# Reordering the handover from the shared feed-forward to the routed experts, and the order of each expert tile's steps

## The reference

```
x  = x + ((x * ys) @ weight) * d                       # ys = cond / sqrt(512)
shared = (silu(x @ w1) * (x @ w3)) @ w2                # hidden width 1024
s = sigmoid([x, cond] @ router_W);  top 2 of 8 by s + bias;  gates = s_sel / sum(s_sel)
routed = sum over the two chosen e of gate * (gelu(x @ W1e[e]) @ W2e[e])   # width 512
out = x + (shared + routed) / 3
```

## Time and profile before

| what | value |
|---|---|
| median of 3 runs (lowest, highest) | 1060.47 us (1059.27, 1061.65) |
| the profiled execution's own time | 1054.4 us |
| its span, first to last instruction | 1052.6 us |
| TensorE busy in the span | 1021.2 us, 97% |
| VectorE, ScalarE, GpSimd busy | 506.2, 293.0, 331.5 us |
| mean granted TensorE clock | 0.996 of full |

### The profile page before, as it was taken

One profiled execution on the slowest core, in us unless ns is written; L12 is line 12 of the kernel. 1 busy time (PEld: TensorE's weight loads), 2 busy tenths in 40 slices (PEclk: granted clock), 3 DMA queues, 4 the chain that ended last, 5 costly groups with the idle time before them and its releaser, 6 DMA issues.

```text
span 1052.6 us, 14602 instructions
## 1 busy us (share of the span) xinstructions
PE 1021.2 (97%) x4692; PEld 836.1 (79%) x4692; DVE 506.2 (48%) x828; ACT 293.0 (28%) x461; POOL 331.5 (31%) x393
## 2 busy tenths in 40 slices
PE   6999999999999999999999998999999999999996
PEld 5888778887888888888888886788888888878874
DVE  4555456668333333333322214555655566555653
ACT  3222252332222222122211112333333233332331
POOL 2000000001214433334312401365554645545533
PEclk9999999999999999999999999999999999999999
DMA  4666688787876677876833576999778999999984
GB/s 172 200 206 217 222 281 255 259 318 248 294 239 233 221 267 253 264 268 212 290 100 90 190 202 205 239 221 231 147 147 179 226 221 231 210 215 226 228 180 80
DMA packets 133259, 228.61 MB, mean 217 GB/s; under 512 B 29041, under 2 KB 83953, under 8 KB 125105
## 3 DMA queue, kind: packets, MB, share of 16 engines
q1 hardware_dynamic: 60400, 144.06, 42.8%
q0 software_dynamic: 31328, 64.11, 26.4%
q10 hardware_dynamic: 41472, 19.68, 7.9%
HBM read 112.85 MB, written 98.38 MB: 201 GB/s over the span
## 4 chain that ended last, share of the span: by engine, by line
PE 83%; DMA 8%; DVE 4%; SPq 2%; issue 2%; ACT 1%; POOLq 0%; DVEq 0%
PE banks L530 13%; PE banks L532 12%; PE banks L531 12%; PE banks L468 8%; PE banks L469 8%; PE banks L470 8%; DMA we_d<-ehl 5%; PE banks L482 4%; PE banks L483 4%; PE banks L484 4%; PE banks L416 3%; PE banks L417 3%; PE banks L418 3%; DMA eraw<-expert_w 2%; SPq L286 1%
## 5 line engine op out<-in xcount | busy, mean ns | idle before, releaser
L468 PE MATMUL banks<-xh,w 128*128 128x512 f32 x512 | 199.6, 390 | 1.8 <-DVE xl L725 1.8
L469 PE MATMUL banks<-xl,w 128*128 128x512 f32 x512 | 199.2, 389 | 0.0
L470 PE MATMUL banks<-xh,w 128*128 128x512 f32 x512 | 199.2, 389 | 0.0
L1184 POOL DMA_INDIRECT out<-ys,slot x71 | 124.0, 1746 | 181.1 <-DVE ys L1080 89.4
L792 DVE SCALAR_TENSOR_TENSOR gm<-sil,banks 128x512 f32<-128x512 f32 x64 | 43.9, 685 | 240.7 <-ACT sil L611 234.6
L1073 DVE TENSOR_TENSOR hidtl<-hidt,hidth 128x512 fp32r<-128x512 f32 x71 | 49.1, 692 | 165.9 <-ACT hidth L685 165.2
L611 ACT ACTIVATE sil<-banks 128x512 f32<-128x512 f32 x64 | 38.2, 597 | 291.9 <-PE banks L470 291.9
L1170 POOL DMA_DIRECT2D xg<-xs_d x136 | 99.9, 1108 | 58.8 <-DVE xgt L1054 49.6
L530 PE MATMUL banks<-we,hidth 128*128 x284 | 112.2, 395 | 5.8 <-issue 5.5
L530 PE MATMUL banks<-we,xgth 128*128 x284 | 111.1, 391 | 3.4 <-issue 3.4
L468 PEld LDWEIGHTS banks<-xh,w 128*128 128x128 f32 x512 | 96.1, 188 | 22.3 <-issue 2.3
(11 more groups left out here) (163 smaller groups left out, 1512.0 us busy)
## 6 DMA issues: line engine op xcount, KB each, us to landing
we_d<-ehl SPq DMA_DIRECT2D x32, 1024.0 KB, 7.3
we<-we_d SPq DMA_DIRECT2D x48, 512.0 KB
hturn<-hid ACTq DMA_DIRECT2D x284, 64.0 KB
xg<-xs_d POOLq DMA_DIRECT2D x136, 128.0 KB
eraw<-expert_w SPq DMA_DIRECT2D x32, 512.0 KB
x1t_d<-x1t SPq DMA_DIRECT2D x8, 1024.0 KB, 8.8
xin<-x1t_d SPq DMA_DIRECT2D x8, 1024.0 KB, 8.8
x_d<-x1tok SPq DMA_DIRECT2D x32, 256.0 KB
```

The costliest lines, as they stand in the source:

```text
L468: pe.matmul(ps[hc % 2][:, :], w_hi, xh[:, j, c, :], start=(c == 0), stop=False)
L469: pe.matmul(ps[hc % 2][:, :], w_hi, xl[:, j, c, :], start=False, stop=False)
L470: last = pe.matmul(ps[hc % 2][:, :], w_lo, xh[:, j, c, :], start=False, stop=(c == DC - 1))
L1184: pool.indirect_dma_start(out[:, :], IO(slot[:, t, 0:1], 0), ys[:, t % RING, :], None, compute_op=ALU.add).then_inc(added[t % 2], 16)
```

## The change

Five things are edited.

- **TensorE.** Block 6 and the first seven steps of block 7 are written out behind a shorter loop. `look_up(0)` goes ahead of `up(7, 7)`, and `matmul1(0)` goes between `down(7, 6)` and `down(7, 7)`. At the end `matmul1(70)` follows `matmul1(69)` directly, ahead of `matmul2(66)`.
- **ACT.** `x_high_of(0)` goes ahead of the last `gate`, `x_high_of(1)` behind the last `gh`. Round t becomes `hidden(t)`, `x_high_of(t + 2)`, `move_h(t)`, `h_high_of(t - 2)`; the wait for `mm1_done` ahead of `x_high_of` is gone, since `hidden(t)` has it. The last `move_h` follows `h_high_of(68)`.
- **DVE.** `turn_x(0)`, `turn_x(1)`, `take_x(0)` go behind step 6 of block 7; `take_x(1)`, `turn_x(2)`, `take_x(2)`, `turn_x(3)` go ahead of `output(7)`. The rounds from 2 on keep their order, except that the last ones have `take_y` last.
- **Memory.** `hturn` moves to where the shared stage's first `xh` buffer was, `hidth` to where `xres` was. So `move_h(0)` no longer waits for `output(7)`, and `h_high_of(0)` does.

The diff, without the place that `x_high_of` was moved from:

```diff
--- before.py
+++ after.py
@@ -99,9 +99,9 @@
         xgth = sb("xgth", [2, DC, P], FP32R, 152)
         xgtl = sb("xgtl", [2, DC, P], FP32R, 156)
         hid = sb("hid", [RING, HE], FP32, 184)
-        hturn = sb("hturn", [RING, SUB, P], FP32, 160)
+        hturn = sb("hturn", [RING, SUB, P], FP32, 128)
         hidt = sb("hidt", [2, DC, P], FP32, 140)
-        hidth = sb("hidth", [2, DC, P], FP32R, 132)
+        hidth = sb("hidth", [2, DC, P], FP32R, 160)
         hidtl = sb("hidtl", [2, DC, P], FP32R, 136)
         ys = sb("ys", [RING, D], FP32, 176)
         xrow = sb("xrow", [XB, ROW], FP32, 192)
@@ -517,9 +517,16 @@
                     down(1, hc - 1)
                 else:
                     down(0, HC - 1)
-            with pe.Fori(1, NBLK // 2) as h:
+            with pe.Fori(1, NBLK // 2 - 1) as h:
                 for j in range(2):
                     shared_block(2 * h + j, j)
+            shared_block(NBLK - 2, 0)
+            for hc in range(HC - 1):
+                up(NBLK - 1, hc, 1)
+                if hc:
+                    down(NBLK - 1, hc - 1)
+                else:
+                    down(NBLK - 2, HC - 1)
 
             def product(ps, high, low, place, m, midway):
 
@@ -555,13 +562,18 @@
                 product(y_ps[t % 2][:, :], hidth[:, t % 2], hidtl[:, t % 2], place, 1, lambda: None).then_inc(mm2_done, 1)
 
             pe.wait_ge(tables_done, 3)
+            look_up(0)
+            up(NBLK - 1, HC - 1, 1)
+            down(NBLK - 1, HC - 2)
             pe.wait_ge(gm_done, HC * NBLK - 1 + 2)
-            look_up(0)
+            matmul1(0)
             down(NBLK - 1, HC - 1)
             pe.wait_ge(gm_done, HC * NBLK + 2)
-            for t in range(TILES + LAG):
-                if t < TILES:
+            for t in range(1, TILES + LAG):
+                if t < TILES - 1:
                     matmul1(t)
+                if t == TILES - 2:
+                    matmul1(TILES - 1)
                 if t == LAG:
                     pe.wait_ge(o_done, SUB * NBLK)
                 if t >= LAG:
@@ -630,8 +642,15 @@
                     act.wait_ge(er_in[j], 16 * half + 16)
                     act.activation(ehl[:, j, 0], eraw[:, j, 1], ACT.Copy).then_inc(eh_ready, 1)
 
+            def x_high_of(t):
+
+                act.wait_ge(xturn_done, t + 1)
+                act.activation(xgth[:, t % 2], xgt[:, t % 2], ACT.Copy).then_inc(xgth_done, 1)
+
             def block_steps(n, j, turn, pieces=True):
                 for hc in range(HC):
+                    if turn is None and hc == HC - 1:
+                        x_high_of(0)
                     gate(n, hc)
                     if turn is not None:
                         next_high(n, hc, j, turn)
@@ -658,11 +677,6 @@
 
             block_steps(NBLK - 1, 1, None, False)
 
...
             def hidden(t):
 
                 act.wait_ge(mm1_done, t + 1)
@@ -684,19 +698,20 @@
                     act.wait_ge(mm2_done, t - 2 + 1 + 1)
                 act.activation(hidth[:, t % 2], hidt[:, t % 2], ACT.Copy).then_inc(hidth_done, 1)
 
-            x_high_of(0)
+            x_high_of(1)
             for t in range(TILES + TURN_LAG):
-                if t + 1 < TILES:
-                    if t:
-                        act.wait_ge(mm1_done, t)
-                    x_high_of(t + 1)
                 if t < TILES:
                     hidden(t)
-                    if t == 0:
-                        act.wait_ge(o_done, SUB * NBLK)
+                if t + 2 < TILES:
+                    x_high_of(t + 2)
+                if t < TILES - 1:
                     move_h(t)
+                if t == TURN_LAG:
+                    act.wait_ge(o_done, SUB * NBLK)
                 if t >= TURN_LAG:
                     h_high_of(t - TURN_LAG)
+                if t == TILES - 1:
+                    move_h(t)
 
 
         @block.vector
@@ -1037,11 +1052,6 @@
                         if hc == 0:
                             output(2 * h + j - 1)
                         piece_low(2 * h + j, hc)
-            for n in (NBLK - 2, NBLK - 1):
-                for hc in range(HC):
-                    block_step(n, hc, n % 2, n < NBLK - 1)
-                    if hc == 0:
-                        output(n - 1)
             def turn_x(t):
 
                 if t % PAIR == 0:
@@ -1059,6 +1069,19 @@
                 dve.wait_ge(xgth_done, t + 1)
                 dve.tensor_tensor(xgtl[:, t % 2], xgt[:, t % 2], xgth[:, t % 2].bitcast(FP32), ALU.subtract).then_inc(xgt_done, 1)
 
+            for n in (NBLK - 2, NBLK - 1):
+                for hc in range(HC):
+                    block_step(n, hc, n % 2, n < NBLK - 1)
+                    if hc == 0:
+                        output(n - 1)
+                    if n == NBLK - 1 and hc == HC - 2:
+                        turn_x(0)
+                        turn_x(1)
+                        take_x(0)
+            for t in range(2):
+                take_x(t + 1)
+                turn_x(t + 2)
+
             def turn_h(t):
 
                 dve.wait_ge(h_moved[t % RING], 16 * (P // Q) * (t // RING + 1))
@@ -1087,23 +1110,22 @@
                 then(dve.tensor_tensor(same[0:1, 1:TILES], wait_for[0:1, 1:TILES], same[0:1, 1:TILES], ALU.subtract))
                 dve.tensor_scalar(wait_for[0:1, 1:TILES], same[0:1, 1:TILES], 16.0, None, ALU.mult).then_inc(waits_done, 1)
 
-            turn_x(0)
-            turn_x(1)
-            take_x(0)
             output(NBLK - 1)
             for t in range(TILES + LAG + 1):
                 if t == 1:
                     dve.wait_ge(slots_in, 16 * SUB)
                     scatter_waits()
-                if t > LAG:
+                if LAG < t < TILES - 1:
                     take_y(t - LAG - 1)
-                if t + 1 < TILES:
+                if 2 <= t < TILES - 1:
                     take_x(t + 1)
-                if t + 2 < TILES:
+                if 2 <= t < TILES - 2:
                     turn_x(t + 2)
                 if 0 <= t - TURN_LAG < TILES:
                     turn_h(t - TURN_LAG)
                     take_h(t - TURN_LAG)
+                if t >= TILES - 1:
+                    take_y(t - LAG - 1)
 
 
         @block.gpsimd
```

More of the change, by code:

```diff
@@ L659, in _ @@
             block_steps(NBLK - 1, 1, None, False)
-            def x_high_of(t):
-                act.wait_ge(xturn_done, t + 1)
-                act.activation(xgth[:, t % 2], xgt[:, t % 2], ACT.Copy).then_inc(xgth_done, 1)
             def hidden(t):
```

## The result

The changed kernel takes 1093.22 us in the median of six runs (1091.31 to 1094.35), the kernel before 1060.72 in six runs beside it (1058.67 to 1065.06). The ratio is 1.0297, with a 95% interval of 1.0276 to 1.0319: slower by 32.5 us, where 1097 us was forecast, slower by 36.5. The profiled execution took 1094.12 us by its own time.

The account below looks back on a forecast made before the run. TensorE, 97% busy, bounds the kernel before; the change adds a longer circle of waits. `take_h(66)` at 1063.8, plus 18.7 and 7.0, gives a span of 1089.5 us, so a median of about 1097, range 1083 to 1120.

Parts of the forecast that it names:

- Part 1, the handover: From `down(7, 6)` to `matmul2(0)`: `matmul2(0)` starts at 657.5 instead of 661.18, 3.7 us gained, a 3.1 us wait left.
- Part 2, the circle: Mid-stage: DVE and ACT wait for each other round by round, 6.18 us against TensorE's 5.44, over 65 rounds 401.7 us.
- five terms: `take_h` to `turn_x` end 2.56, DVE to ACT 0.04, `x_high_of` to DMA 0.10, DMA to `h_high_of` 2.81, to `take_h` 0.67.
- the fourth term: In each mid-stage round, from the start of the first DMA to the start of `h_high_of`: 2.81 us.
- rows 8 to 11: Profile rows of the kernel before: DVE's sequencer behind a waiting `take_y(69)`, ACT's loop counter behind a waiting `gh`.
- first rival: Mid-stage: ACT's sequencer goes past a waiting `x_high_of`, so no circle; only handover and end count, 1053.8 us; chance 0.11.
- second rival: Mid-stage: DMAs can't start while ACT computes, so each round has 0.53 us more, 1131 us; chance 0.08.
- Part 3, the end: After `take_h(66)`: a small gain, 18.7 us to the last matmul's end, the old end's two waits (2.3 and 0.4) gone.
- nothing changes: Behind the last matmul, `take_y(70)`, the last scatter and its landing stay as before, 7.0 us to the span's end.
- The sum: Whole kernel: span 1089.5 us against 1052.6 before, +36.9; with 6.1 us from profiled execution to median, about 1097 us.

Follow-up runs that it names:

- `turn_x` ahead: The changed kernel with DVE's `turn_x` one tile further ahead, `turn_x(t + 3)` in round t; 1060.67 us, 1.0021.
- the same with the loads earlier: The changed kernel with `turn_x` one tile further ahead and POOL loading each pair of tiles' x rows one scatter sooner; 1056.77 us, 0.9979.
- the longer circle: The changed kernel with DVE's `turn_h(t - 2)` moved ahead of `turn_x(t + 2)`; 1130.22 us, 1.0673.
- the old end again: The changed kernel with `take_y` behind `turn_x`, and the end of the kernel before; 1057.08 us, 0.9977, and in a second run 1054.27 us, 0.9949.

## Why the prediction was right

Direction, mechanism and size held: 1093.22 us lies in the range, 4 us under the forecast. Step by step:

- **Part 1, the handover.** The gain was to be 3.7 us with one wait of 3.1 left; it is 3.9 (23.10 to 19.24) with one of 2.9 from start to start (2.62 of it idle). But all of it starts 3.3 us later than forecast, `down(7, 6)` at 641.42 for 638.08. That isn't the change: in this execution TensorE's clock fell twice for a stretch to its lower level, 1.2 GHz, shortly after a wait of 1.84 us that ended at 115.75 and again after one of 2.08 us that ended at 139.99. The rows are the kernel before and then the changed one, with the same work in that stage, first around 115 and then around 140 us:

```profile
113.00:123.00 10.00, 8.16 (x91) 6.40 (x84) 5.26 (x8) 2.94 (x3) 0.00 (x0) 1.00 0.75 260
```
```profile
113.00:123.00 10.00, 8.16 (x56) 6.21 (x48) 4.87 (x7) 2.35 (x2) 0.00 (x0) 0.83 0.81 264
```
```profile
138.00:148.00 10.00, 9.97 (x44) 8.28 (x45) 7.41 (x10) 6.40 (x10) 0.00 (x0) 1.00 0.85 275
```
```profile
138.00:148.00 10.00, 8.01 (x28) 6.49 (x29) 7.60 (x10) 7.10 (x10) 0.00 (x0) 0.83 0.79 286
```

The same matmuls run 1.6 us later than in the kernel before from 119 us on and 3.6 us later from 142 us on; by the end of the stage it is 3.3.

- **Part 2, the circle.** 65 rounds took 398.1 us, 6.124 each, for 401.7 and 6.18 forecast. All five terms are there: 2.57, 0.04, 0.01, 2.85 and 0.66 us in the mean, for 2.56, 0.04, 0.10, 2.81 and 0.67. The one that was mis-sized is the third, `x_high_of` to the first DMA: 0.006 us in 66 rounds for 0.10. It was read from a sequencer that goes past a running instruction, while here it stands at the waiting one and goes on with it; 0.135 us is seen only in the first three rounds, where `x_high_of` doesn't wait. 65 x 0.09 = 6 us is too much for the whole difference of 3.6: the fourth term, with the DMAs of some rounds longer (3.54 us at 869.61), gave 2 back. The DMAs at 661.56 took 4.24 us, ahead of the 65 rounds, and probably moved `take_h(1)` by the 1.1 us that it is late.
- **What decided it.** ACT's sequencer stops at an `x_high_of` whose semaphore hasn't come, as rows 8 to 11 had it in other places. The rule of the Trainium skill (Perfetto Trace Analysis, Per-engine timelines), by which the wait stands in a queue and the sequencer goes on, would have given the first rival's 1054 us. No run here agrees with it: in each of the 66 rounds in which `x_high_of` waits, the DMAs stand behind it, though `hid` is ready, and taking them out from there (`x_high_of` last) brings the time to 1056.33 us. The second rival, DMAs only once `x_high_of` is done, falls by the same rows: the first DMA begins 0.01 us after it.
- **Part 3, the end.** `take_h(66)` to the last matmul's end: 18.82 us for 18.7. Behind it "nothing changes" was wrong: 8.9 us for 7.0. The last `matmul2` now follow each other every 2.7 us and the last three scatters stand 3.0 and 3.5 us apart, which the run of the end alone shows by itself. The prediction had left the scatters' own distance out.
- **The sum.** Span: 641.42 + 25.08 + 398.08 + 18.82 + 8.9 = 1092.3 us, for 638.08 + 24.0 + 401.7 + 18.7 + 7.0 = 1089.5. The errors of +3.3, +1.1, -3.6, +0.1 and +1.9 us leave +2.8 of some 10 in all, and that they offset each other is luck. The forecast then added 6.1 us for the distance of the median from the profiled execution of before; this time the median is 0.9 us below the profiled execution (1093.22 to 1094.12), so this term was 7.0 us too large. +2.8 and -7.0 give the 4 us. The prediction thought of busier queues for this distance; a part of it goes with TensorE's clock. Of 29 timed runs of the kernel before, beside the experiment with ACT's order alone, the 15 with a mean granted clock of 0.995 or more have a median of 1057.4 us, the other 14 one of 1062.0; on the three other chips the same division gives 1.3 to 3.0 us. The profiled execution of before had 0.996, that of the changed kernel 0.993.

The version that beats both kernels by most is the changed one with `take_y` behind `turn_x`: 0.994 and 0.9944, about 6 us under the kernel before by the ratios, 5 by the medians. The profile puts 3.9 us of it into the handover; mid-stage is unchanged (5.52 us a round for 5.54), and the rest isn't told apart. The two profiled spans don't show the gain (1052.5 and 1052.6 us), since this execution too reaches `down(7, 6)` 3.6 us late, with the clock at 0.83 around 115 and 140 us; the timed runs do.

## What to carry to other kernels

Before a step is moved, follow each wait back through the queues of all engines for one round: if the chain comes back to the same step one round later, its length is a second bound beside the busiest engine, however idle its members look. Each half microsecond by which it is longer than the busiest engine's time costs half a microsecond in every round, here 65 times, and what isn't needed inside the circle (here `take_y`) belongs behind the step that the other engine waits for. DMA issues count as part of such a chain, since they stand behind whatever waits ahead of them on their queue.

## What the runs showed that I had not expected

A DMA that stands behind a waiting ACT instruction is started 0.006 us after that instruction starts; behind one that doesn't wait it takes 0.135 us. So ACT need not be idle for its sequencer to start a DMA.

TensorE's clock fell to 1.2 GHz shortly after a wait of 1.84 us that ends near 115 us (granted 0.83 from 113 to 123 us), after one of about 2 us near 140 us (0.83 from 138 to 148 us in the changed kernel), or after both, in 12 of the 14 profiled executions. In the kernel before, with waits of 1.84 and 1.74 us in these places, and in the run of the end alone it fell after neither. In five executions it also fell around the wait ahead of `matmul2(0)` (granted 0.83 from 658 to 668 us with ACT's order alone, `turn_x` ahead, the same with the loads earlier, and the longer circle; 0.72 with the old end again). The many short waits in mid-stage, 0.47 us each as the profile counts them, left it at 1.00 over 372 us in the changed kernel. In the longer circle, with 64 of 1.0 us, it fell once near 989 us (0.83 from 985 to 995 us), which is why its 372 us stand at 0.99. Why a like wait does it in one execution and not in another stays open.
